# Four engine orders of a software-pipelined attention, written anew

## What is computed

```python
K = jnp.einsum('bpd,ihd->biph', x, W_K)
Q = jnp.einsum('bpd,ihd->biph', x, W_Q)
V = jnp.einsum('bpd,ihd->biph', x, W_V)
scores = jnp.einsum('biph,biqh->biqp', K, Q)
scores = jnp.where(mask[None, None, :, :], scores, NEG_INF)
attn = jax.nn.softmax(scores / np.sqrt(d_head).astype(np.float32), axis=-1)
z = jnp.einsum('biph,biqp->biqh', V, attn)
z_flat = jnp.transpose(z, (0, 2, 1, 3)).reshape(b, q_len, -1)
out = jnp.einsum('bqf,df->bqd', z_flat, W_O)
```

## Time and profile before

| | |
|---|---|
| Median of the runs | 690.81 us (689.43 to 691.62, three runs) |
| The profiled execution | 687.63 us |
| Its span | 685.80 us |
| Busy share of the span | PE 96%, DVE 89%, ACT 79%, POOL 71% |
| Attention | from about 142 us to the end |

### The profile page before, as it was taken

How to read it: one execution, slowest core, us unless ns; L and a number is a source line. 1 busy time by engine, 2 the same in 40 slices (tenths; PEclk the granted TensorE clock), 3 DMA queues, 4 the chain that set the end, 5 groups by cost and what they waited for, 6 DMA issues and landing times.

```text
span 685.8 us, 14711 instructions
## 1 busy us (share of the span) xinstructions
PE 658.9 (96%) x4589; PEld 593.5 (87%) x4589; DVE 613.1 (89%) x1657; ACT 544.1 (79%) x1280; POOL 487.1 (71%) x494
## 2 busy tenths in 40 slices
PE   8779999979999999999999999999999999999997
PEld 7669999958889899999888999988889999897886
DVE  8977777768999999999999999999999999998996
ACT  4745555568888888898898989888888889888883
POOL 5274343257697878787887878697978787979871
PEclk9879999999999999999999999999999999999999
DMA  7614632207071524242533424243516151616001
GB/s 229 194 30 110 159 91 57 42 27 162 7 172 34 133 57 115 61 106 60 119 89 78 111 60 97 70 96 83 130 40 140 32 139 29 142 29 161 5 29 34
DMA packets 50235, 61.01 MB, mean 89 GB/s; under 512 B 7440, under 2 KB 28272, under 8 KB 50160
## 3 DMA queue, kind: packets, MB, share of 16 engines
q1 hardware_dynamic: 47856, 55.36, 33.5%
q0 software_dynamic: 2304, 4.72, 2.8%
HBM read 12.87 MB, written 4.72 MB: 26 GB/s over the span
## 4 chain that ended last, share of the span: by engine, by line
PE 67%; DVE 6%; POOL 4%; issue 1%; ACT 1%; POOLq 0%; ACTq 0%
PE ps_big L1383 17%; PE ps_mid L1418 17%; PE ps_z L1439 7%; PE ps_z L1438 7%; PE ps_misc L1251 5%; PE ps_misc L1253 4%; PE ps_misc L1252 4%; PE ps_big L1439 3%; PE ps_big L1438 3%; DVE ps_big L1110 2%; DVE pT_lo L1157 2%; POOL probs L691 2%; POOL z_lo L696 1%; POOL k_st L702 1%; DVE z_sum L1165 1%
## 5 line engine op out<-in xcount | busy, mean ns | idle before, releaser
L691 POOL TENSOR_TENSOR probs<-probs,rden 128x1024 f32<-128x1024 f32 (+7 forms) x256 | 294.2, 1164 | 96.0 <-DVE rden L1146 95.0
L864 ACT ACTIVATE pT_hi<-ps_mid 128x512 fp32r<-128x512 f32 (+3 forms) x384 | 184.5, 493 | 53.2 <-PE ps_mid L1418 47.9
L1157 DVE TENSOR_TENSOR pT_lo<-ps_mid,pT_hi 128x512 fp32r<-128x512 f32 (+3 forms) x384 | 206.8, 550 | 10.4 <-ACT pT_hi L864 7.9
L1110 DVE CUSTOM_DVE_ANT_0 ps_big<-ps_big,later 128x1024 f32<-128x1024 f32 (+7 forms) x256 | 194.3, 759 | 10.2 <-PE ps_big L1383 8.2
L851 ACT ACTIVATE probs<-ps_big,neg_max 128x1024 f32<-128x1024 f32 (+7 forms) x256 | 190.3, 743 | 4.2 <-DVE neg_max L1110 3.4
L1383 PE MATMUL ps_big<-k_st,q_st 128*128 128x512 f32 (+2 forms) x768 | 193.3, 363 | 0.1
L1418 PE MATMUL ps_mid<-ident,probs 128*128 128x128 f32 x1152 | 179.7, 275 | 6.0 <-DVE pT_lo L1157 4.7
L1418 PEld LDWEIGHTS ps_mid<-ident,probs 128*128 128x128 f32 x1152 | 131.8, 140 | 27.8 <-issue 15.1
L1383 PEld LDWEIGHTS ps_big<-k_st,q_st 128*128 128x128 f32 x768 | 124.3, 189 | 13.1 <-ACT probs L851 2.0
L1438 PE MATMUL ps_z<-pT_hi,v_st 128*128 128x256 f32 x448 | 116.5, 290 | 0.0
L1439 PE MATMUL ps_z<-pT_lo,v_st 128*128 128x256 f32 x448 | 112.9, 282 | 0.0
(11 more groups left out here) (242 smaller groups left out, 1213.6 us busy)
## 6 DMA issues: line engine op xcount, KB each, us to landing
k_st<-k_st SPq DMA_DIRECT2D x90, 256.0 KB, 3.8
q_st<-q_parts SPq DMA_DIRECT2D x128, 128.0 KB, 3.1
y_dram<-y_sb SPq DMA_DIRECT2D x40, 64.0 KB
k_st<-k_parts SPq DMA_DIRECT2D x8, 256.0 KB
raw_gu<-in_L_ffn_Wg_dram SPq DMA_DIRECT2D x9, 176.0 KB, 3.0
raw_gu<-in_L_ffn_Wu_dram SPq DMA_DIRECT2D x9, 176.0 KB, 3.1
raw_d<-in_L_ffn_Wd_dram SPq DMA_DIRECT2D x9, 128.0 KB, 2.9
res<-in_L_attn_x_dram SPq DMA_DIRECT2D x4, 256.0 KB, 3.5
```

Of the source, the lines that this page charges most:

```text
L691: pool.tensor_tensor(rows, rows, col.to_broadcast([P, width]), ALU.mult).then_inc(normed, 1)
L864: nc.scalar.activation(pT_hi[:, t:t + 2 * tiles - 1:2, :], ps_mid[:, bank, 0:tiles * P].rearrange("p (t q) -> p t q", t=tiles), ACT.Copy). ...
L1110: nc.vector.tensor_tensor_reduce(cols, cols, later[:, S - width:S], 1.0, FLOOR, ALU.add, ALU.min, neg_max[:, n:n + 1]).then_inc(max_done, 1)
L1157: nc.vector.tensor_tensor(pT_lo[:, at, :], ps_mid[:, bank, 0:tiles * P].rearrange("p (t q) -> p t q", t=tiles), pT_hi[:, at, :].bitcast(F3 ...
```

## The change

The four order texts are replaced. Every step of a list is in it again, once; offsets, `MISC_ORDER`, `UNITS` and `JOBS` are as before, and no operation, wait or transfer is added or removed. The steps of the gathers hang on the count of `N` steps, whose order among themselves is the same.

```diff
--- before.py
+++ after.py
@@ -303,21 +303,20 @@
 
 
         PE_ORDER = read("""
-            V5.0- S3 V5.1- Mq1 T15.0- S4 T0.0 T0.1 S5 V6.0- V6.1- T1.0 V6.2- T2.0 S6 T2.1 Mk1 V7.0- S7 T3.0 Mv0
-            T4.0 S8 V0.0 T4.1 Mv2 S9 V0.1 T5.0 Mv3 T6.0 S10 V0.2 S11 T6.1 Mo1- V1.0 T7.0 Mv1 S12 T8.0 V2.0 T8.1
-            Mo0- V2.1 T9.0 S13 Mwo S14 V3.0 Mwqkv+ T10.0 T10.1 S15 V3.1 Mk0+ T11.0 T12.0 S0+ Mq0+ T12.1 V4.0 S1+
-            V4.1 T13.0 S2+ T14.0 T14.1""")
+            Mq1 V5.0- V5.1- T15.0- S3 T0.0 S4 T0.1 V6.0- S5 V6.1- T1.0 V6.2- S6 T2.0 T2.1 Mk1 V7.0- S7 T3.0 Mv0 T4.0 S8
+            V0.0 Mv2 T4.1 V0.1 S9 T5.0 Mv3 V0.2 S10 T6.0 T6.1 Mo1- V1.0 S11 T7.0 Mv1 S12 T8.0 V2.0 T8.1 Mo0- V2.1 T9.0
+            S13 Mwo S14 T10.0 T10.1 Mwqkv+ S15 V3.0 V3.1 T11.0 Mk0+ S0+ T12.0 T12.1 V4.0 Mq0+ S1+ T13.0 V4.1 S2+ T14.0
+            T14.1""")
         ACT_ORDER = read("""
-            H14.0- H14.1- E2 H15.0- Cq1 E3 H0.0 H0.1 E4 H1.0 Z2- H2.0 E5 H2.1 Ck1 E6 H3.0 Cv0 H4.0 E7 Z3- H4.1
-            Cv2 E8 Y1- H5.0 Cv3 E9 H6.0 Y0- E10 H6.1 H7.0 Cv1 E11 H8.0 H8.1 E12 H9.0 Cwo E13 Z0 Cwqkv+ H10.0
-            H10.1 E14 Ck0+ H11.0 E15 H12.0 Z1 H12.1 E0+ H13.0 E1+ Cq0+""")
+            H14.0- H14.1- E2 H15.0- Cq1 E3 H0.0 H0.1 E4 H1.0 E5 Z2- H2.0 H2.1 Ck1 E6 H3.0 Cv0 Z3- H4.0 E7 Cv2 Y1- E8
+            H4.1 H5.0 Cv3 E9 H6.0 H6.1 E10 Y0- H7.0 Cv1 E11 H8.0 E12 H8.1 H9.0 Cwo Z0 E13 H10.0 H10.1 Cwqkv+ E14 H11.0
+            Ck0+ Z1 H12.0 E15 H12.1 E0+ H13.0 Cq0+ E1+""")
         DVE_ORDER = read("""
-            Cq0 L14.0- X3 L14.1- R1 L15.0- R2 X4 Cq1 L0.0 L0.1 R3 X5 L1.0 R4 Z2- X6 L2.0 L2.1 X7 R5 Ck1 R6 L3.0
-            Cv0 X8 L4.0 L4.1 R7 Cv2 X9 Z3- R8 L5.0 Cv3 X10 L6.0 Co1- X11 R9 L6.1 L7.0 Cv1 X12 R10 L8.0 R11 Co0-
-            L8.1 R12 X13 L9.0 Cwo X14 R13 Cwqkv+ L10.0 L10.1 X15 Z0 R14 Ck0+ L11.0 X0+ R15 L12.0 X1+ L12.1 Z1
-            L13.0 X2+ R0+""")
+            X2 L14.0- L14.1- X3 R1 L15.0- R2 Cq1 X4 L0.0 X5 L0.1 L1.0 R3 R4 X6 Z2- L2.0 L2.1 R5 X7 R6 L3.0 Ck1 Cv0 X8
+            L4.0 Z3- Cv2 R7 X9 R8 L4.1 L5.0 Cv3 X10 L6.0 Co1- R9 L6.1 X11 L7.0 R10 Cv1 X12 L8.0 Co0- R11 R12 L8.1 X13
+            L9.0 Cwo X14 L10.0 Cwqkv+ L10.1 Z0 X15 R13 R14 L11.0 Ck0+ X0+ L12.0 R15 L12.1 Z1 R0+ X1+ L13.0 Cq0+""")
         POOL_ORDER = read("""
-            N1 N2 N3 N4 K0 N5 N6 K1 Z1- N7 N8 Z0- N9 N10 N11 N12 N13 N14 N15 N0+""")
+            N1 N2 K0 N3 N4 N5 N6 Z1- K1 N7 N8 Z0- N9 N10 N11 N12 N13 N14 N15 N0+""")
 
         MISC_ORDER = ["wqkv", "k0", "q0", "q1", "k1", "v0", "v2", "v3", "o1", "v1", "o0", "wo"]
         OUTS = [int(n[1]) for n in MISC_ORDER if n[0] == "o"]
```

## The result

The changed kernel takes 705.79 us, median of four runs (704.68 to 708.04), beside 691.21 us (689.43 to 692.13) for the kernel before on the same chip. The ratio is 1.0241, 95% interval [1.0207, 1.0275]: slower by 2.4%, some 14.6 us by the medians and 16.6 us by the ratio.

What follows compares the result with a forecast made beforehand. TensorE (96% busy) and VectorE (89%) were taken as both full. Terms 16.8 + 5.6 - 5.7 = +16.7 us on the profiled 687.63 gave 704.3, so a median of 707.5 us; 8-in-10 range 686 to 716.

Steps and rivals of the forecast that it cites:

- part two: VectorE's casts Ck0 and Ck1, in their new places behind GpSimd's multiplications, wait: 16.8 + 5.6 us lost.
- three terms: Ck0's wait, 16.8 us lost; Ck1's wait, 5.6 us lost; the new order's removed TensorE waits, 5.7 us gained.
- part one: New order removes TensorE waits at S11 and Mo1: 0.51 us in 7 halves without values, 0.3 in 7 with; 5.7 gained.
- A cast behind GpSimd waits to the end: VectorE's cast issued during GpSimd's multiplication waits for its end: near 1.8 us for Ck0, 1.3 for Ck1.
- `Ck0` costs 1.2 us in each of 14 halves, 16.8 in all: Ck0 behind L11.0, issued with about 1.35 us of N14 to go, delays X0 and so T13.0: 16.8 us.
- The first rival: At both casts: the cast doesn't wait (one SBUF input, or slips between two GpSimd operations); 685.1 us, faster; chance 0.17.
- the second: Rival: casts wait, but GpSimd is still in N13 or N5; loss no more than 5.7 us, about 691; chance 0.08.
- `Ck1` costs 0.7 in halves with values and 0.1 without, 5.6 us: Ck1 behind R6 L3.0 waits 0.9 us for N6, delaying Mv2 with values, T5.0 and T6.0 without: 5.6 us.
- The second way to the sum: VectorE waits of 2.25 us per half against 1.7 us idle: 698.5 us if idle time absorbs them, 716.6 if none.

Runs made afterwards that it cites:

- the casts at home: Changed kernel with both casts put where GpSimd has nothing running (Ck1 directly behind R5, Ck0 ahead of R14), rest of the new order kept: 688.36 us, ratio 0.9976.
- the casts moved: Kernel before with only the casts moved, Ck1 to behind R6 L3.0 and Ck0 to behind L11.0: 704.77 us, ratio 1.0229.
- the reduction: Changed kernel, orders as they are, keys rounded by tensor_reduce over one element instead of the cast: 688.79 us, ratio 0.9974.
- the run with `Ck0` at home: Changed kernel with Ck0 alone back ahead of GpSimd's multiplication (R13 L11.0 Ck0 R14 X0), Ck1 still late: 699.07 us, ratio 1.0122.
- With `Ck1` at home: Changed kernel with Ck1 alone back directly behind R5, Ck0 still behind L11.0: 697.32 us, ratio 1.0122.
- Three experiments: GpSimd's new list alone in the kernel before, 1.006; changed kernel with both casts home plus Z2 behind Ck1, 1.0006, or plus V3.0 ahead of T10.0, 0.9996.

## Why the prediction was right, and where it wasn't

The forecast was slower, 707.5 us; it is 705.8. The mechanism of part two is shown by the casts at home, the casts moved and the reduction. That the number is so near is luck: none of the three terms held. `Ck0` had 16.8 us and was worth 6.7 to 10.3, `Ck1` had 5.6 and was worth 8.2 to 10.3, and part one took off 5.7 where 0 to 1.7 were left. The errors nearly cancel.

*A cast behind GpSimd waits to the end.* Right: 2.00 us for `Ck0` and 1.49 for `Ck1`, where 1.8 and 1.3 were expected. The rule of the Trainium skill, page "SBUF — State Buffer", section "Who interferes with whom", agrees with the trace as far as the cast goes: its end is 0.28 us behind the end of GpSimd's instruction in both. The cast was issued earlier into GpSimd's instruction than forecast, 0.18 us into `N14` and 0.05 into `N6` instead of 0.55 and 0.35, so it waited longer. `N14` took 1.90 us where it ran first, as expected, and 2.07 where the cast got in ahead of it.

*`Ck0` costs 1.2 us in each of 14 halves, 16.8 in all.* The price per wait was near (1.41 at `T13.0`), but the number of halves was not: the step took one pattern, `N14` already running, for all halves. It left out that `R13` now stands next to `R14`, so `N13` runs first, with `N14` behind it. In every other half the cast is in time for the gap between them. That is 7 x 1.41 = 9.9 us; the run with `Ck0` at home gave 6.7 to 10.3. The first rival named the way (the cast slips in between two of GpSimd's operations) and the second named `N13`, both as a case for all casts; it holds for 7 of the loop's 29 casts.

*`Ck1` costs 0.7 in halves with values and 0.1 without, 5.6 us.* 0.85 at `Mv2` was measured, so the first term holds. The second failed. `T5.0` and `T6.0` came 0.83 to 0.85 us late, and the argument that `T10.0` waits for GpSimd anyway covers only a third of it: `T10.0` waits 0.27 us less in both halves than with the casts at home (0.24 and 0.10 instead of 0.51 and 0.38), and `T11.0` 0.10 less in one of them. With `Ck1` at home 8.2 to 10.3 us came back. The waits of the casts thus cost 17.4 to 20.4 us together, where the forecast had 22.4.

*Part one gives back 5.7 us.* This is the step that failed. The waits at `S11` and `Mo1` did go, with another at `S9` that the prediction hadn't seen, and `Mo1` follows its transpose at once. These waits were 0.77 and 0.80 us in the halves without values, more than the 0.51 of the forecast, and at most 0.02 in the halves with values, where it had taken 0.3: 5.6 us in 14 halves, so their sum was right by luck too. But with the casts at home only 1.7 us of gain are left by the ratio (1.2 by the medians, 0.6 by the stretch), and in the four windows nothing. In their place stand `T10.0` (costed at 0.14 and left out of the sum; 0.38 to 0.51 in the halves without values, nothing in the others), `S15`, `T11.0`, `T0.0` and `T3.0`: the sum of waits of four halves is 5.83 us against 5.84. The prediction added up stalls of TensorE as if each were a gain by itself, although it had just read that VectorE is idle only 1.7 us per half. Three experiments took such a wait away, and in each the same amount or more turned up within the same half (0.37 at `Mo1` to 0.89 at `T7.0`; 0.3 at `T3.0` to 0.4 at `T4.1` and 0.46 at `Mv2`; `T10.0` and `S15` to `T11.0`, with all waits together at 6.5 us of four halves, more than the 5.83 without the edit). The first of these was started from the kernel before, where it was GpSimd's own new order that made `T7.0` wait. The term should have been 0 to 1.7.

*What VectorE's idle time takes in.* The second way to the sum bounded this between all and nothing, though its lower end, 698.5, left out the 5.7 us that the upper end takes off. Casts cost 7.5 us more per four halves (10.8 us instead of 3.3) and the halves grew by 5.84, so about a quarter was absorbed. VectorE's idle time fell by 2.5, but 1.8 of that is there with both casts at home too.

*The first rival*, that a cast doesn't wait because it has only one input in SBUF, is refuted by the 21 casts that waited. But the count of inputs isn't what decides: the reduction has the same input and output and doesn't wait.

## What to carry to other kernels

An order written by hand can hold pairs of instructions that must not meet. Here VectorE's cast from SBUF to SBUF has to be issued while GpSimd is idle or just before it is released, or be replaced by an operation that ran beside GpSimd without a wait (the reduction), even if that is slower by itself; in a place one or two instructions later it cost up to nearly GpSimd's whole multiplication. And where two engines are as full as here, a stall of one of them can't be booked as a gain before it is known that the other can make the next step earlier too.

## What the runs showed of the chip

- Whether the cast waits is settled at the boundary between two of GpSimd's instructions. Issued during the first of two that run back to back, it goes ahead of the second (0.43 us at 377.85, issued 0.14 us before `N13` ended; 0.90 at `Ck1` of the kernel before with casts moved, where it waits for the end of `N5` alone). Issued in the second, even 0.05 us after its start, it waits for all that is left (1.49 us at 393.65, 2.00 at 343.32).
- A reduction with the cast's operands takes 0.68 us instead of 0.42 and ran beside GpSimd's multiplication with no effect on either. The cast first, GpSimd second, costs GpSimd 0.10 us (`N5` in the kernel before) to 0.18 (`N14` and `N6` behind a cast that got in), less than what is left of the cast.
- A cast that waited holds up what GpSimd does next as well: the small multiplication behind `N14` and `N6` takes 0.58 us there (at 345.00 and 394.81), and 0.40 behind `N6` with the reduction.
- The waiting is recorded as busy time: 28 casts count 36.8 us instead of 11.7. VectorE's share of the span stands at 91% with it, at 90% with both casts at home and at 89% before.
- The part ahead of attention varied from execution to execution: `S8` of the first half came between 152.9 and 158.5 us in kernels that do the same there, so small differences between kernels are better read from the stretch behind it.
